# Half-row projection pairs in the scores' tiling, one accumulator, a fifth probability buffer and one sum step on TensorE, in a differential-attention block

## What is computed

```python
qkv = layernorm(x) @ w_qkv;  q, k, v = split(qkv)        # 16 heads of 32
q1, q2 = split(q, 2);  k1, k2 = split(k, 2)              # halves of 16
a = softmax(q1 k1^T * scale) - lam * softmax(q2 k2^T * scale)
out = a @ v;  out = out / rms(out) * norm_w * 0.2
x = x + reshape(out) @ wo
h = bitlinear(layernorm(x), w_fc) + gate * low_rank(layernorm(x))
x = x + bitlinear(relu(h)**2, w_proj)                    # ternary weights
```

## Time and profile before

| | |
|---|---|
| median of 3 runs | 3939.27 us (3936.23 to 3948.39) |
| the profiled execution | 3940.3 us, span of the profile 3938.6 us |
| busy share of the span | TensorE 96%, VectorE 81%, ScalarE 71%, GpSimd 3% |
| start until the first pair's tail | about 179 us |
| pairs with projections and after, to pair 55 | some 2283 us |
| last eight pairs, tail, feed-forward part | 342, 96, 1039 us |

### The profile page before, as it was taken

The page is one execution under the profiler, slowest core; times in us unless marked ns, Lnnn a source line. Parts: engine busy times, 40 slices in busy tenths (PEclk is TensorE's granted clock), DMA queues, the critical chain, the costliest instruction groups (busy, mean ns, idle before and its releaser), DMA issues.

```text
span 3938.6 us, 57545 instructions
## 1 busy us (share of the span) xinstructions
PE 3774.7 (96%) x21960; PEld 2070.1 (53%) x21960; DVE 3205.4 (81%) x3089; ACT 2782.0 (71%) x3597; POOL 99.5 (3%) x78
## 2 busy tenths in 40 slices
PE   6799999999999999999999999999889999999999
PEld 5344444444444444444444444333378888888887
DVE  5699999999999999999999999988855555555554
ACT  2688888888888888888888888988733333333333
POOL 0000000000000000000000000000000000000000
PEclk9899999999999999999999999999989999999999
DMA  5545444445444445444444445433101010101010
GB/s 196 129 101 114 99 112 108 102 107 111 111 99 114 108 96 121 104 108 104 108 106 107 112 93 115 103 74 90 48 10 43 22 43 22 43 22 43 22 43 22
DMA packets 225844, 338.24 MB, mean 86 GB/s; under 512 B 86704, under 2 KB 107184, under 8 KB 225008
## 3 DMA queue, kind: packets, MB, share of 16 engines
q1 hardware_dynamic: 225520, 333.88, 34.7%
HBM read 180.72 MB, written 150.99 MB: 84 GB/s over the span
## 4 chain that ended last, share of the span: by engine, by line
PE 65%; DVE 22%; ACT 5%; issue 5%; DMA 1%; SPq 1%; DVEq 0%; ACTq 0%
DVE acc L1222 17%; PE ps L589 13%; PE ps L689 12%; PE ps L669 12%; PE ps L564 10%; PE ps L506 5%; PE ps L645 4%; PE ps L503 3%; ACT pr L921 3%; PE ps L610 2%; PE ps L674 1%; DVE stg L1155 1%; PE ps L719 1%; DVE ot L1234 1%; PE ps L709 1%
## 5 line engine op out<-in xcount | busy, mean ns | idle before, releaser
L921 ACT ACTIVATE pr<-ps 128x1024 f32<-128x1024 f32 x2048 | 1989.7, 1032 | 278.4 <-PE ps L564 272.3
L1222 DVE TENSOR_TENSOR acc<-acc,pr 128x2048 f32<-128x2048 f32 x752 | 1736.5, 2309 | 39.5 <-ACT pr L921 16.0
L589 PE MATMUL ps<-pr,vst 128*32 128x512 f32 x8192 | 1023.3, 601 | 0.0
L564 PE MATMUL ps<-qst,kst 50*128 50x512 f32 x4096 | 800.0, 460 | 58.9 <-ACT pr L921 38.0
L564 PEld LDWEIGHTS ps<-qst,kst 50*128 50x128 f32 x4096 | 339.3, 184 | 730.8 <-ACT pr L921 515.5
L1075 ACT ACTIVATE rb<-ps,scf 128x512 f32<-128x512 f32 x256 | 176.7, 690 | 388.4 <-PE ps L674 388.4
L589 PEld LDWEIGHTS ps<-pr,vst 128*32 128x32 f32 x8192 | 208.5, 109 | 429.2 <-issue 423.8
L689 PE MATMUL ps<-tP,hh_ 128*128 128x512 f32 x1024 | 404.4, 395 | 1.9 <-DVE hl_ L1442 1.9
L669 PE MATMUL ps<-yh,tT 128*128 128x512 f32 x1024 | 404.5, 395 | 0.0
L669 PE MATMUL ps<-yl,tT 128*128 128x512 f32 x1024 | 399.5, 390 | 0.0
L689 PE MATMUL ps<-tP,hl_ 128*128 128x512 f32 x1024 | 399.1, 390 | 0.0
(11 more groups left out here) (154 smaller groups left out, 3493.6 us busy)
## 6 DMA issues: line engine op xcount, KB each, us to landing
qst<-q_scratch SPq DMA_DIRECT2D x128, 384.0 KB, 6.3
kst<-k_scratch SPq DMA_DIRECT2D x128, 384.0 KB, 9.6
q_scratch<-stg SPq DMA_DIRECT2D x168, 256.0 KB
k_scratch<-stg SPq DMA_DIRECT2D x168, 256.0 KB
xin<-in_L_attn_x_dram SPq DMA_DIRECT2D x16, 1024.0 KB, 5.4
v_scratch<-vsg SPq DMA_DIRECT2D x64, 256.0 KB, 3.1
vst<-v_scratch SPq DMA_DIRECT2D x128, 128.0 KB, 5.4
xr<-in_L_attn_x_dram SPq DMA_DIRECT2D x64, 256.0 KB
```

The lines of the kernel that those rows point to most:

```text
L564: ins = e.matmul(ps[:, 2 * c + hh, :], kst[rows, r, j, t * 128:(t + 1) * 128], qst[rows, r, j, c * 512:(c + 1) * 512], start=True, stop=True)
L589: ins = e.matmul(ps[32 * c4:32 * c4 + 32, 4 + j, :], vst[:, r, t, 32 * hh:32 * hh + 32], pr[:, sl, c, hh, :], start=(t == 0), stop=(t == 7 ...
L921: e.activation(pr[:, sl, c, :, :], ps[:, 2 * c:2 * c + 2, :], ACT.Exp, scale=SCALE).then_inc(s_exp, 1)
L1222: e.tensor_tensor(acc[:, j, :], old, new, ALU.add).then_inc(s_add, 1)
```

## The change

- The projections' and output projection's matmuls are cut in halves of 64 rows (`pe_tile_half`, `pe_wo_half`) and issued in pairs, one half at rows 0 to 63 and one at rows 64 to 127, in the same tiling as the scores (`pe_halves`). While one tile's upper rows are done in one bank, the tile before has its lower rows done in the other (`TILE_BANK`: 6, 7, 6; the output projection in 7). `SLOTS` gives the pairs of each step. A tile so ends at step 3, 5 or 7 instead of 1, 3 or 5, and its bank is waited for at steps 0, 2, 4 and 6.
- Transposes (`pe_turn`, the post transposes) and `pe_flag` 0 move ahead of a step's first scores, behind the products.
- The sums go to banks 5 and 4, the products' own. There is one accumulator `acc`; the first add of each half waits for the sum of the half before.
- TensorE adds slot 7 of each pair by ones (`pe_sum_step`, at step 4); slot 15 of the last eight pairs goes back to VectorE. `pe_sum_0` and `pe_sum_1` stand ahead of the step's products.
- `NPB` is 5; the products run one slot later.
- The square goes from GpSimd to ScalarE. Copies, layer norm steps, bounds, flags, stores and loads move by some half steps to match; in the last eight pairs the ternary weights' transposes go to steps 0, 2, 3 and 4 of the next pair.

```diff
-RING, NPB = 2, 4
+RING, NPB = 2, 5
...
+SLOTS = (8, 4, 6, 6, 8, 4, 6, 6)
+TILE_BANK = (6, 7, 6)
+TERNARY = (0, 2, 3, 4)
...
+    return 13 * P + 6 * j + max(t, 1)
+def split_wo(X):
+    return 0 <= X and 3 * (X + 2) + 24 < 24 * B
...
-    if d == 6:
-        return C, r, 4
-    if d == 2 and r == 1:
-        return C, 0, 5
+    if d == 7:
+        return C, (0, 2, 3)[r - 1]
+    if d == 0 and r == 2:
+        return C, 1
...
-                e.tensor_tensor(sq[:], on[:], on[:], ALU.mult).then_inc(s_osq, 1)
...
+                    if d == 0 and P and 3 * P + 21 < 24 * B:
+                        sync_store(e, 3 * P + 23)
+                    if d == 0 and P:
+                        sync_load_v(e, P, 1)
...
+        def pe_tile_half(e, T, h, n):
+            C, i = divmod(T, 12)
+            a = T % 3
+            rows = slice(64 * h, 64 * h + 64)
+            k, part = divmod(n, 3)
+            if h == 0 and n == 0:
+                if a == 1 and T > 33:
+                    e.wait_ge(s_x2v, (T - 24) // 3 - 2)
...
+                elif T > 24:
+                    tile_read(e, T - 2 if a == 2 else T - 1)
...
+            w = (wqh, wql, wqh)[part]
+            xx = (xth, xth, xtl)[part][:, C % 2]
...
+            if i < 8:
+                m0 = TILES[i] * 128
+                t = e.matmul(ps[:, TILE_BANK[a], :], w[rows, k, m0:m0 + 128], xx[rows, k, :], start=begin, stop=end)
...
+            if end:
+                t.then_inc(s_tile, 1)
+        def pe_wo_half(e, X, h, n):
+            rows = slice(64 * h, 64 * h + 64)
+            kk, i = divmod(n, 3)
+            if h == 0 and n == 0:
+                e.wait_ge(s_otl, X + 1)
+                e.wait_ge(s_wol, 1)
+                tile_read(e, 24 + 3 * (X + 2) + 1)
+            o_, w_ = ((oth, woh), (oth, wol), (otl, woh))[i]
+            t = e.matmul(ps[:, 7, :], o_[rows, kk, :], w_[rows, kk, :], start=(h == 0 and n == 0), stop=(h == 1 and n == 11))
+            if h == 1 and n == 11:
+                t.then_inc(s_owo, 1)
+        def pe_halves(e, P, d):
+            n0 = SLOTS[d - 1] if d % 2 else 0
+            T = 24 + 3 * P
+            for n in range(n0, n0 + SLOTS[d]):
+                if T < 24 * B:
+                    if d < 6:
+                        pe_tile_half(e, T + d // 2, 0, n)
+                    elif split_wo(P - 2):
+                        pe_wo_half(e, P - 2, 0, n)
+                    if d >= 2:
+                        pe_tile_half(e, T + d // 2 - 1, 1, n)
+                if d < 2 and split_wo(P - 3):
+                    pe_wo_half(e, P - 3, 1, n)
...
+                if gg:
+                    e.wait_ge(s_rln, 2 * P + j)
...
+        def pe_sum_step(e, P):
+            gg = 16 * P + 7
+            e.wait_ge(s_exp, n_half(gg, 1))
...
+                e.wait_ge(s_raw, P)
...
+            pe_ones(e, 5, pr[:, gg % NPB].rearrange("p c h n -> p (c h n)"), True, False)
+        def pe_sum_0(e, P):
+            e.wait_ge(s_add, n_add(P, 0, 6))
+            pe_ones(e, 5, acc[:], False, True).then_inc(s_sum, 1)
+        def pe_sum_1(e, X):
+            e.wait_ge(s_add, n_add(X, 1, 7))
...
+            e.wait_ge(s_xtl, turned(X + 1))
+            if (X + 1) % NP == NP - 1 and X + 2 < NPAIR:
+                e.wait_ge(s_flv, 6 * ((X + 1) // NP + 1) + 3)
+            pe_ones(e, 4, acc[:], True, True).then_inc(s_sum, 1)
...
+                    if d == 1 and P:
+                        pe_sum_1(e, P - 1)
+                    if d == 5:
+                        pe_sum_0(e, P)
                     if gg >= 4:
+                        pe_pv(e, gg - 4)
+                    if gg >= 4 and not last:
                         pe_pv(e, gg - 3)
-                    if d == 1 and P:
-                        pe_sum(e, P - 1, 1)
-                    if d == 5:
-                        pe_sum(e, P, 0)
-                    last = 3 * P + 24 >= 24 * B
-                    if gg >= 2 and not last:
-                        pe_pv(e, gg - 2)
...
+                        pe_sum_step(e, P)
+                    if q == NP - 1 and P + 1 < NPAIR and d == 0:
+                        pe_flag(e, P // NP + 1, 0)
+                    if turn_at(P, d):
...
+                        pe_turn(e, *turn_at(P, d), 4)
+                    if not last:
+                        pe_posts(e, P, d)
                     pe_score(e, P, k, 1)
                     pe_score(e, P, k + 1, 0)
+                    pe_halves(e, P, d)
                     if last:
-                        pe_pv(e, gg - 2)
-                    if d in PIECES and 3 * P + 24 < 24 * B:
-                        a, n0, n1 = PIECES[d]
-                        T = 24 + 3 * P + a
...
-                        pe_tile(e, T, 6, n0, n1)
-                    if q == NP - 1 and P + 1 < NPAIR:
...
-                    if turn_at(P, d):
...
-                        pe_turn(e, *turn_at(P, d))
-                    pe_posts(e, P, d)
...
+                        pe_pv(e, gg - 3)
+                        pe_posts(e, P, d)
+                    if P > NPAIR - NP and d in TERNARY:
+                        pe_ternary(e, P - (NPAIR - NP) - 1, TERNARY.index(d))
...
                     pe_score(e, P, k + 1, 1)
                     if gg + 2 < NSLOT:
                         pe_score(e, (gg + 2) // 16, (gg + 2) % 16, 0)
...
+                    if q == NP - 1 and P + 1 < NPAIR and d == 2:
+                        pe_flag(e, P // NP + 1, 1)
...
+                    if f % 16 == 7:
+                        e.wait_ge(s_sum, 2 * (f // 16) + 1)
...
+            if d == 3 and half == 1:
...
+            if d == 4 and half == 0:
+                e.wait_ge(s_raw, X + 1)
+                if X:
+                    e.wait_ge(s_ssq, X)
+                e.activation(sq[:], on[:], ACT.Square).then_inc(s_osq, 1)
...
+                    if d in (3, 5, 7) and more:
+                        act_tile(e, 24 + 3 * P + d // 2 - 1, TILE_BANK[d // 2 - 1])
...
-            if t == 0 or (t == 7 and pe_adds(P)):
+            if t == 0 or k == 7:
...
+                if 2 * P + j:
+                    e.wait_ge(s_sum, 2 * P + j)
...
+            e.tensor_tensor(acc[:], old, new, ALU.add).then_inc(s_add, 1)
...
-            steps = {(1, 1): (0,), (2, 0): (1,), (3, 0): (2,), (4, 0): (3,), (5, 0): (4,), (6, 1): (6,), (7, 0): (7,),
-                     (7, 1): (8,)}
-            rest = {(0, 0): (9,), (0, 1): (10,)}
+            steps = {(2, 0): (0,), (2, 1): (1,), (3, 0): (2,), (4, 0): (3,), (5, 0): (4,), (6, 1): (6,), (7, 0): (7,)}
+            rest = {(0, 1): (8,), (1, 0): (9,), (2, 0): (10,)}
...
+                        if d in (3, 5, 7) and half == 1 and more:
+                            dve_low(e, 24 + 3 * P + d // 2 - 1, TILE_BANK[d // 2 - 1])
+                        if (d, half) in ((4, 1), (6, 1)) and more:
+                            dve_bound(e, 24 + 3 * P + d // 2 - 2)
+                        if (d, half) == (0, 1) and P and 3 * P + 21 < 24 * B:
+                            dve_bound(e, 24 + 3 * P - 1)
...
+                        if q == NP - 1 and P + 1 < NPAIR and (d, half) in ((0, 0), (0, 1), (3, 0)):
+                            dve_flag(e, P // NP + 1, half if d == 0 else 2)
```

More of the change, by code:

```diff
@@ L620, in pe_sum @@
-            t.then_inc(s_sum, 1)
+                    c4, q0 = 2 * hh + c, (2 * c + hh) * 512
+                    t = e.matmul(ps[32 * c4:32 * c4 + 32, bk, :], ones[:], cols[:, q0:q0 + 512], start=start, stop=stop,
+                                 skip_group_check=True)
+            return t
+        def pe_sum_step(e, P):
+            gg = 16 * P + 7
+            e.wait_ge(s_exp, n_half(gg, 1))
+            if P:
+                e.wait_ge(s_raw, P)
+            else:
+                e.wait_ge(s_xtl, 12)
+            pe_ones(e, 5, pr[:, gg % NPB].rearrange("p c h n -> p (c h n)"), True, False)
@@ L939, in act_post @@
                 act_sum_exp(e, X, 1)
-            if d == 4 and half == 0:
+            if d == 3 and half == 1:
                 e.wait_ge(s_tr, X + 1)
@@ L1228, in dve_post @@
             p = X % NP
-            if d == 1 and half == 0:
+            if d == 1 and half == 1:
                 e.wait_ge(s_rex, 2 * X + 2)
@@ L1237, in dve_post @@
                 e.tensor_tensor(ot[:], ot[:], rl[:, 0, :], ALU.add).then_inc(s_ot, 1)
-            if d == 5 and half == 1:
+            if d == 4 and half == 1:
                 e.wait_ge(s_osq, X + 1)
@@ L1244, in dve_post @@
                     .then_inc(s_ssq, 1)
-            if d == 7 and half == 1:
+            if d == 6 and half == 1:
                 e.wait_ge(s_rmex, X + 1)
@@ L1249, in dve_post @@
                     .then_inc(s_on, 1)
-            if d == 9 and half == 1:
+            if d == 10 and half == 1:
                 e.wait_ge(s_oth, X + 1)
@@ L1253, in dve_post @@
                     .then_inc(s_otl, 1)
-            if d == 16 and half == 0:
+            if d == 17 and half == 1:
                 e.wait_ge(s_owo, X + 1)
```

221 lines of the change are left out of this document (84 added, 137 removed).

## The result

The changed kernel takes 4107.62 us (median of 4 runs, 4105.07 to 4109.16), beside 3943.83 for the kernel before on the same chip: a ratio of 1.0416, interval 1.0393 to 1.0438. The direction was forecast, the size was not: 4029 was forecast with 4060 as the upper end, so 79 us of the 164 were missed.

What follows compares the result with a forecast made beforehand. Bound: two exponentials and hand-overs, 2.97 us from scores to products; VectorE in mod-0 pairs. Sum: 3940.3 + 64 (fours) + 4 (pairs 52 to 55) + 22 (batch ends) - 2 (last eight) + 1.5 (tail) = 4029.8, said 4029; range 3940 to 4060.

Steps and rivals of the forecast that it cites:

- The exponentials hold the step: In each step, two exponentials and hand-overs take 2.97 us from scores to products, already hiding the projections to within some hundredths.
- The sixteen switches less in a pair: TensorE's mode switches, two of 0.20 in each of eight steps: 3.2 us less work a pair, close to no gain.
- The rival in which the switches come through: Exponentials don't hold the second scores, pairs cost their engines' work: some 3800 us, half of it 3870; together chance 0.12.
- the one with serial halves: Rival: the two halves of each half-row pair run one after the other, 0.46 a pair: 4360 us; chance 0.04.
- Together the chain changes by -0.39 - 0.39 + 1.18 + 0.86 = +1.26 a pair: Per pair: eight-matmul step 2 and turn's transposes each save 0.39; transposes ahead of scores add 1.18, sum step 0.86.
- One wait of 3 at each batch end: At a batch's last pair, step 0, the flag matmul waits 3.2 us for VectorE's flag operation; seven times, +22.
- The stalls in the fours, +4.9 each: TensorE waits of 1.3, 1.9, 0.6 and 0.85 us raise four pairs to 174.0; thirteen fours, +64.
- 1.3 and 1.9 for the tile's bank: Mod-0 pairs (P mod 4 = 0): projections wait for VectorE at step 4 (1.3) and the next pair's step 0 (1.9).
- 42.93, 0.6 and 0.85: Chain of a pair with two turns, mod-1's wait at next step 0, and the sum's wait for mod-2's step-0 turn.
- The reason given for the stalls: With one accumulator each half's first add waits for the previous half's sum, holding up VectorE's later operations that free banks.
- The start, 0 forecast: The stretch before the first tail; the prediction's sum has no term for it.
- The prediction's 42.7 for a pair of these: Mean time in us taken for each of the last eight pairs in the kernel before; change there forecast at -2.

Runs made afterwards that it cites:

- e1: Changed kernel with only 5 of each tile's 12 half-row pairs made, for projections and output projection: 4088.98 us, ratio 1.0378 to the kernel before.
- e3: Changed kernel with each exponential over 384 of 512 columns from the fifth slot on: 4075.1 us, ratio 1.0343 to the kernel before.
- e6: Changed kernel with the turn's and tail's transposes back behind the half-row pairs, ahead of the second scores: 4085.09 us, ratio 1.0354 to the kernel before.
- e9: Changed kernel without TensorE's sum step, slot 7's sum back on VectorE: 4117.96 us, ratio 1.0456 to the kernel before.
- e5: Changed kernel with both flag matmuls at the end of step 0 in bank 4, VectorE's flag operations at step 0: 4044.24 us, ratio 1.0258.
- e10: Kernel before with one accumulator instead of two, four buffers, all else as before: 4001.27 us, ratio 1.0159.
- e13: Changed kernel with two accumulators and its five buffers kept; output projection loses its high part for room: 4110.75 us, ratio 1.0418 to the kernel before.
- e17: Changed kernel with mod-0 pairs' statistics moved behind the subtraction at step 3 and to step 4, mod-1 pairs' turns to steps 6 and 7: 4077.02 us, ratio 1.0349.
- e18: e17 with the flags placed as in e5 and the transposes as in e6: 4028.98 us, ratio 1.0224 to the kernel before.

## Why the prediction was right in direction and wrong in size

**The exponentials hold the step: right, and shown.** The 2.97 returned to the hundredth, e1 shows that the projections can be cut by more than half for 19 us, and e3 that shorter exponentials take 2.7 from a mod-3 pair and nothing from a mod-0 pair, which waits for VectorE. The sixteen switches less in a pair bought nothing, as forecast. The rival in which the switches come through is out; so is the one with serial halves.

**"Together the chain changes by -0.39 - 0.39 + 1.18 + 0.86 = +1.26 a pair": nearly right.** Mod-3 pairs were forecast at 42.34 and took 42.6; e6 puts the transposes at 0.7 to 0.8 there (0.79 by the terms), e9 the sum step at 0.5 (0.86 by the terms). That mod-2 pairs took nothing from e6, and mod-1 pairs 0.4 more, is not explained; over all ordinary pairs the transposes' place is worth nothing.

**"One wait of 3 at each batch end", 7 x 3.2 = 22: the step that failed most.** The wait before the flag was sized well, 3.4 against 3.2. The second wait was overlooked: `pe_post` waits for the flag's copy, since the flag's second matmul now sits in the bank that the post transposes overwrite, and that costs 3.7. It can be read off the kernel, as a line added to `pe_post` (L680). These two make 7.1 of the 9.8 in the two pairs shown (95.1 against 85.3); the other 2.7 go with a clock of 0.96 in both windows. The forecast had no term for that. By e5 all of it is 63 us (74 by the windows): at least 41 of the 79 missed.

**The stalls in the fours, +4.9 each: measured 6.5 over the same 169.1.** Mod 0 was forecast at 44.95 and took 45.2, which is partly luck: the working had 1.3 and 1.9 for the tile's bank on a chain of 41.75, the trace has 2.6 in all and 42.6 for the rest. The mod-1 interval is where it fell short. It holds the turn at step 0 of the mod-2 pair and came out at 45.1; the forecast's 42.93, 0.6 and 0.85 make 44.4. The turn waits twice: 0.85 for the sum behind it was right (0.8), but the turn itself first waits 0.9 for VectorE to have read the turn before, in the same bank. The chain's 0.3 in each of the other pairs is the rest. Some 20 us of the miss in all.

**The reason given for the stalls was half wrong.** The prediction starts VectorE's lateness from the single accumulator. In the kernel before that is true (e10, +62). In the changed kernel it isn't: with two accumulators nothing changes (e13), and VectorE is idle for the same 3.4 in a mod-0 pair. What counts there is how much VectorE has ahead of the subtraction (e17, 1.4 of the pair). The costs of the parts do not add up: e10's 62, e5's 63 and e6's 22 come near to the 164, but taking the accumulator back in the changed kernel yields 0, and e6 yields 8 once e5 is in, since it too gained at the batch ends.

**The start, 0 forecast: +9.7 in this profile.** The window of the first pair, from 136, takes 52.9 at a clock of 0.87, where the kernel before takes 43.2 at 1.00:

```profile
136.00:179.20 43.20, 39.02 (x255) 15.68 (x248) 42.55 (x38) 36.10 (x44) 0.00 (x0) 1.00 0.47 103
```

The profiles of all kernels built on the kernel before have the start at 179.0 to 183.6, those built on the changed one at 184.5 to 189.2. So a part of it is the change's; its cause wasn't tried. With pairs 52 to 55 (3.4 off beside the flags) and the tail (0.7) this covers the rest; the last eight went 7 the other way, which was not looked into. The prediction's 42.7 for a pair of these was from the row of pairs 55 to 62; it is 43.2 (345.6 / 8), which leaves the sum as it is.

**Left open.** After e18, 90 us remain over the kernel before: in the pairs, about 0.7 (mod 3), 1.3 (mod 2) and 2.2 (mod 1), and 4.4 in the mod-2 pair of six batch ends. Products a slot later, the banks shared by sums and products, and the staggering over two banks were not undone one at a time.

## What to carry to other kernels

Find what the step waits for before pricing what is taken out of it: sixteen mode switches saved are worth nothing beside an exponential that takes as long. For each bank or buffer that gets a second use, list every instruction that must now wait, and walk that list for the rare paths (a batch's end) too: here one such line cost as much as all the forecast had put there. And when VectorE is full, move work off it only together with its order: the same add taken away made the kernel 0.4% slower in one order and 0.3% faster in another, and 0.5% with a second one.
